# Ones-products of the softmax denominators moved beside the weighted sums, on one Trainium2 core

## The chip, the cores and the metric

The program runs on one core of one Trainium2 chip. The metric is device time in microseconds. The kernel before takes 1741.16 us (median of 3 runs, 1738.98 to 1742.28).

## The reference, cut to what matters

A two-layer network on x of 16 x 256 x 512 and a context of the same shape. Each layer is a cross attention and a feed-forward part. The change touches the attention of the second layer, eight heads of 32 channels over 512 positions:

```python
def _L1_xattn_ref(q, k, v, gamma):
    # q: layernorm(x), k and v: context, all [16, 256, 512]
    qh, kh, vh = (t.reshape(B, 8, 32, 512) for t in (q, k, v))
    qk = jnp.einsum('bhdq,bhdl->bhql', qh, kh) / sqrt(32)
    sm = jax.nn.softmax(qk, axis=-1)
    ret = jnp.einsum('bhql,bhdl->bhdq', sm, vh).reshape(B, 256, 512)
    return gamma * ret
```

The softmax denominators are the sums of exp(qk) over the 512 keys. Around it, for every batch, stand a latent attention with its own 512 x 512 softmax, a base and low-rank layer (together called the preparation of a batch here), and behind it the routing into a mixture of 64 experts, whose phase starts when all 16 batches are done.

## The kernel before, in words

**Slots.** The second attention is cut into 512 slots, 32 for a batch. A slot is one head and one block of 128 keys. Four heads form a half; four slots of four heads, one for each key block ("a step"), make 4 x 4 = 16 slots, called a quad: 32 quads in all. In slot n TensorE makes the key product (`key_chunk`, L686) and a score product 20 slots ahead of its turn (`score_chunk`, L677), whose maximum VectorE takes (L1192). ScalarE makes the exponential of the key product into `p_t` (L956), of which there are two buffers, one for each odd and even step. After each step come the weighted sums (`weighted`, L698), four products of 32 columns, one for each head, that share the array. They stand at n + 6.75 for n = 0, 4, 8, 12 of the quad, that is at slots 6.75, 10.75, 14.75 and 18.75.

**Denominators.** They are made by products with a matrix of ones, again four of 32 columns each. GpSimd adds steps 0 and 1 of a quad into `p_sum` (L1442). `sums0` (L713) multiplies `p_sum`, `sums2` the buffer of step 2 and `sums1` that of step 3 (both L720), all into one PSUM bank. ScalarE takes the logarithm of it (`sums`, L968) and the exponential of its negative (`expand`, L972). VectorE multiplies the weighted sums by that (`inv`, L1208), which frees their bank, and adds the result to x (`add`, L1214).

**Order.** Every engine executes one fixed list. `schedule` gives each piece of work a place on a common scale of slots and sorts by place, then by rank: key, score, weighted, tail and maxima, preparation, dispatch. The tail offsets count from the end of a quad (slot 16), so -4 is slot 12 and 0.25 is slot 16.25, which is also slot 0.25 of the next quad. The preparation of a batch is spread over 38 slots and its places count modulo 32; two batches' preparation overlap. Within the 32 slots of a batch, TensorE's pieces that matter here are:

- slots 11 to 15: `s3` (11, L600), `g` (11.75, L592), the maxima's transpose `max` (12, L709), from the third batch of slots on `place` (12, L750 to L753), `t0` and `t1` (13, 13.25, L606), `t2` (14.25), `lat0` (14.75, L613), `t3` (15). `t0` waits for `prob`, which ScalarE normalises in `n2`, `n3` (12.25, 12.5, L890) behind the cast of the maxima `max_hi` (12.25, L963); VectorE's reciprocals `r2`, `r3` (L1095) precede them.
- slots 19 to 24: `lat1` to `lat3` (L613), then `mean` (24.25, L620), which waits for VectorE's `moments` (place 22, L1098, L1100), itself behind ScalarE's `lat` (21.25, L897).
- slots 28 to 34: `max` (28), `o0` and `o1` (28.25, L628), which wait for ScalarE's `relu` (28, L900), and `x0`, `x1` (33, 34.25, L634), which wait for `xn20`, `xn21` (31.25, 32.25, L853).
- slots 36 to 38: `lora` (36, L642), the base products (L655) and `gated` (37, L649), which waits for VectorE's `lora2`, `gates0`, `gates1` (36.25 to 36.75) with ScalarE's `gate_exp` (36.5, L915, L916) between.

A planner (`use`, `taken`) gives banks 5 to 7 to the preparation, tail and dispatch stages in the order of TensorE's list, each time the bank that was last read earliest. So moved places also change which bank a stage gets.

Of the kernel before, what the change touches and what calls it, by code (L numbers as in the profile page):

```python
# [67 lines left out]
GPSIMD_OUT = {"rstd": 14.25, "send": 63}  # L68
SYNC_OUT = {"out": 10}

TENSOR_TAIL = {"sums0": -4, "sums2": -3.5, "sums1": 0.25}
SCALAR_TAIL = {"sums": 0.75, "expand": 2.75}
VECTOR_TAIL = {"inv": 4, "add": 5.5}

TENSOR_MAX = {"max": 1}
SCALAR_MAX = {"max": 1.25}
# [10 lines left out]
def schedule(dims, prepare, tail, maxima, dispatch, core):  # L87

    B, HALF, NHEAD, C = dims["B"], dims["HALF"], dims["NHEAD"], dims["T"] // P
    H4 = NHEAD // HALF
    QUAD, SLOTS = C * H4, NHEAD * C
    AHEAD = LEAD * H4
    out = []
    if "fill" in core:
        late = dims["NEXP"] - FIRST_FILLS
        out += [(prepare["k0"] - PREPARE, 0, ("fill", n)) for n in range(FIRST_FILLS)]
        out += [(FILL_FROM + n * FILL_SLOTS / late - PREPARE, 0, ("fill", FIRST_FILLS + n)) for n in range(late)]
    for n in range(B * SLOTS):  # L100
        if "key" in core:
            out.append((n, 0, ("key", n)))
        if "score" in core:
            out.append((n - AHEAD, 1, ("score", n)))
        if "add" in core and n // H4 % C == 1:
            out.append((n + 1, 2, ("add", n)))
        if "weighted" in core and n % H4 == 0:
            out.append((n + WEIGHTED, 2, ("pv", n // H4)))
    for quad in range(B * HALF):
        out += [(QUAD * (quad + 1) - AHEAD - 1 + o, 3, ("tail", quad, what)) for what, o in maxima.items()]  # L110
        out += [(QUAD * (quad + 1) + o, 3, ("tail", quad, what)) for what, o in tail.items()]
    for b in range(B):
        out += [(SLOTS * b - PREPARE + o, 4, ("prep", b, what)) for what, o in prepare.items()]
        for what, o in dispatch.items():
            for n in range(HALF * dims["TOPK"] if what == "send" else 1):
                out.append((SLOTS * (b + 1) + o + n, 5, ("disp", b, what, n)))
    return [(at, ev) for at, _, ev in sorted(out, key=lambda x: x[:2])]
# [22 lines left out]
def build(nc, a, out, slots_dram, dims):  # L140
# [22 lines left out]

    tensor_order = schedule(dims, TENSOR, TENSOR_TAIL, TENSOR_MAX, TENSOR_OUT, ("key", "score", "weighted"))
    scalar_order = schedule(dims, SCALAR, SCALAR_TAIL, SCALAR_MAX, SCALAR_OUT, ("key",))
    vector_order = schedule(dims, VECTOR, VECTOR_TAIL, VECTOR_MAX, VECTOR_OUT, ("score",))
    gpsimd_order = schedule(dims, GPSIMD, {}, {}, GPSIMD_OUT, ("add",))
# [1387 lines left out]
```

## Time and profile before

| | |
|---|---|
| median of the timed runs | 1741.16 us |
| span of the profiled execution | 1799.6 us |
| TensorE busy | 1593.1 us (89%) |
| VectorE busy | 1191.2 us (66%) |
| ScalarE busy | 971.3 us (54%) |
| GpSimd busy | 953.5 us (53%) |
| slots with their preparation | to about 1140 us of the span |
| expert phase | from about 1200 us on |

The profiled execution is 58 us longer than the median of the timed runs. A busy share is an average; what decides is the order within 32 slots, which repeats 14 times with full preparation.

### The profile page before, as it was taken

To read this page: it belongs to the slowest core of one execution; us is meant where nothing else is said; L and a number is where in the kernel's file an instruction comes from. 1 tells how busy PE (TensorE), PEld (TensorE's weight loads), DVE (VectorE), ACT (ScalarE), POOL (GpSimd) and SP (SyncE) were. 2 spreads that over 40 slices of the span, in tenths; PEclk is the share of its full clock that TensorE was granted. 3 is DMA by queue.
4 is the path that set the end of the run, shared out by engine and by line. 5 is a ranking of instruction groups with operands and counts; after the bars stand their busy time and mean duration, and the time that the engine had idled before them with its cause. 6 is when DMAs were issued, how large, how long until landed. Compare 5 with 4: busy or idle time off the path is not lost.

```text
span 1799.6 us, 25136 instructions
## 1 busy us (share of the span) xinstructions
PE 1593.1 (89%) x8144; PEld 1022.0 (57%) x8144; DVE 1191.2 (66%) x2674; ACT 971.3 (54%) x1938; POOL 953.5 (53%) x889
## 2 busy tenths in 40 slices
PE   5799999989999999999999988329998999999995
PEld 2444454444454454444444443229987888888884
DVE  2477778767767877877877865217765767666652
ACT  3345665655655665665665635115554555555552
POOL 4122326455464455455455446556666666666665
PEclk8889999999999999999999989659999999999997
DMA  9957654363363363352342230059999999999995
GB/s 330 303 150 254 229 144 129 121 187 112 124 210 110 116 193 103 101 168 84 89 136 65 58 99 23 21 182 245 253 255 245 254 258 247 255 250 268 245 237 82
DMA packets 148337, 311.91 MB, mean 173 GB/s; under 512 B 27674, under 2 KB 37786, under 8 KB 148208
## 3 DMA queue, kind: packets, MB, share of 16 engines
q1 hardware_dynamic: 109296, 238.89, 42.8%
q0 software_dynamic: 38912, 71.43, 18.1%
q8 instruction: 65, 1.06, 0.2%
q14 instruction: 64, 0.52, 0.1%
HBM read 141.25 MB, written 155.91 MB: 165 GB/s over the span
## 4 chain that ended last, share of the span: by engine, by line
PE 46%; DMA 20%; issue 12%; DVE 10%; another core or an unknown queue 3%; SPq 3%; ACT 3%; POOL 2%; DVEq 1%; POOLq 0%; ACTq 0%
DMA out_rows<-y_slots,row_ids 18%; PE bank L686 7%; PE bank L698 6%; PE bank L677 5%; PE bank L655 3%; PE bank L720 3%; PE bank L600 2%; DVE max_col L1192 2%; SPq L484 2%; PE bank L613 2%; PE bank L606 2%; PE bank L628 2%; POOL out_rows L1501 2%; PE bank L739 1%
## 5 line engine op out<-in xcount | busy, mean ns | idle before, releaser
L1192 DVE TENSOR_REDUCE max_col<-bank 128x1 f32<-128x512 f32 x512 | 340.2, 682 | 148.8 <-PE bank L677 142.0
L956 ACT ACTIVATE p_t<-bank 128x512 f32<-128x512 f32 x512 | 294.3, 596 | 206.7 <-PE bank L686 183.3
L1501 POOL DMA_INDIRECT out_rows<-y_slots,row_ids x128 | 222.6, 1739 | 203.3 <-DMA out_rows<-y_slots,row_ids 160.9
L1454 POOL DMA_INDIRECT slot_rows<-row,slot_i x256 | 255.0, 996 | 77.6 <-issue 76.9
L686 PE MATMUL bank<-q_stack,k_stack 98*128 98x512 f32 x512 | 277.1, 544 | 4.9 <-ACT p_t L956 4.1
L1442 POOL TENSOR_TENSOR p_sum<-p_t 128x512 f32<-128x512 f32 x128 | 168.3, 1320 | 195.9 <-ACT p_t L956 194.0
L677 PE MATMUL bank<-k_stack,q_stack 96*128 96x512 f32 x512 | 212.9, 417 | 4.6 <-DVE max_col L1192 4.3
L686 PEld LDWEIGHTS bank<-q_stack,k_stack 98*128 98x128 f32 x512 | 97.6, 192 | 191.4 <-issue 163.3
L1491 POOL TENSOR_TENSOR down_lo<-down,down_hi 96x1024 fp32r<-96x1024 f32 x64 | 188.4, 2944 | 15.3 <-DVE down_hi L1350 15.3
L1319 DVE TENSOR_TENSOR x_slots_t_lo<-bank,x_slots_t_hi 128x512 fp32r<-128x512 f32 x128 | 88.3, 690 | 160.6 <-ACT x_slots_t_hi L1008 160.6
L795 PE MATMUL bank<-gate_up_hi,x_slots_t_hi 128*128 128x384 f32 x512 | 186.1, 364 | 0.6 <-DVE x_slots_t_lo L1319 0.5
L796 PE MATMUL bank<-gate_up_lo,x_slots_t_hi 128*128 128x384 f32 x512 | 174.6, 341 | 0.0
L797 PE MATMUL bank<-gate_up_hi,x_slots_t_lo 128*128 128x384 f32 x512 | 174.5, 341 | 0.0
L1028 ACT ACTIVATE y_slots<-bank,x_slots 128x512 f32<-128x512 f32 x128 | 88.1, 688 | 128.3 <-PE bank L819 125.3
L1340 DVE TENSOR_TENSOR gate_up_lo<-gate_up,gate_up_hi 128x768 fp32r<-128x768 f32 x128 | 142.7, 1116 | 7.2 <-issue 7.2
L698 PE MATMUL bank<-p_t,v_t 128*32 128x512 f32 x1024 | 140.7, 622 | 0.2 <-DVE head_sb L1208 0.2
L784 PE MATMUL bank<-ident,x_slots 128*128 128x128 f32 x512 | 80.7, 281 | 66.1 <-DMA x_slots<-slot_rows 65.8
L655 PE MATMUL bank<-base_w,x_t 128*128 128x512 f32 x256 | 129.8, 620 | 0.0
L677 PEld LDWEIGHTS bank<-k_stack,q_stack 96*128 96x128 f32 x512 | 99.0, 194 | 53.0 <-issue 29.3
L1371 POOL TENSOR_SCALAR row_rstd<-row_mv 128x2 f32<-128x2 f32 x48 | 10.9, 228 | 199.3 <-DVE row_mv L1078 199.3
L784 PEld LDWEIGHTS bank<-ident,x_slots 128*128 128x128 f32 x512 | 62.9, 143 | 91.1 <-DMA x_slots<-slot_rows 40.0
L1038 ACT CAST gate_up_hi<-gate_up 128x768 fp32r<-128x768 f32 x128 | 105.4, 824 | 13.4 <-DMA down<-in_down 13.4
(178 smaller groups left out, 3246.5 us busy)
## 6 DMA issues: line engine op xcount, KB each, us to landing
gate_up<-in_gate_up SPq DMA_DIRECT2D x64, 768.0 KB
slot_rows<-row SPq DMA_DIRECT2D x64, 577.0 KB, 8.0
x_slots<-slot_rows SPq DMA_DIRECT2D x64, 577.0 KB
k_stack<-prob SPq DMA_DIRECT2D x192, 128.0 KB, 3.8
down<-in_down SPq DMA_DIRECT2D x64, 384.0 KB
q_stack<-x_t SPq DMA_DIRECT2D x128, 128.0 KB
x<-in_x SPq DMA_DIRECT2D x16, 512.0 KB, 3.6
ctx<-in_ctx SPq DMA_DIRECT2D x16, 512.0 KB, 4.5
```

The lines of the kernel that those rows point to most:

```text
L655: e.matmul(bank[:, :], x_t[:, k, c, :], base_w[:, c, :], start=c == 0, stop=False)
L677: e.matmul(psum[2 + n % 2][:, :], q_st[b % 2][0:SK, head, c * P:(c + 1) * P], k_st[b % 2][0:SK, head, :], start=True, stop=True).then_inc( ...
L686: e.matmul(psum[n % 2][:, :], k_st[b % 2][0:SKM, head, j * P:(j + 1) * P], q_st[b % 2][0:SKM, head, :], start=True, stop=True).then_inc(fu ...
L698: m = e.matmul(psum[4][h * DQ:(h + 1) * DQ, :], v_t[b % 2][:, j, head + h, :], p_t[step % 2][:, h, :], start=j == 0, stop=j == C - 1)
L795: e.matmul(bk[:, 0:2 * INNER], xt_hi[u % 3][:, c, :], gu_hi[nw][:, c, :], start=c == 0, stop=False)
L796: e.matmul(bk[:, 0:2 * INNER], xt_hi[u % 3][:, c, :], gu_lo[nw][:, c, :], start=False, stop=False)
L797: m = e.matmul(bk[:, 0:2 * INNER], xt_lo[u % 3][:, c, :], gu_hi[nw][:, c, :], start=False, stop=c == C - 1)
L956: e.activation(p_t[step % 2][:, h, :], psum[n % 2][:, :], ACT.Exp, scale=SCALE).then_inc(free[n % 2], 1)
L1192: e.tensor_reduce(max_col[quad % 2][:, h, c:c + 1], psum[2 + n % 2][:, :], X, ALU.max, negate=True).then_inc(free[2 + n % 2], 1)
L1454: e.indirect_dma_start(out=slots_dram, in_=rows[b % 2][:, k, :], in_offset=None, out_offset=bass.IndirectOffsetOnAxis(ap=slot_i[b % 2][:, ...
L1491: e.tensor_tensor(dn_lo[nw][:, :, :], dn[i][:, :, :], dn_hi[nw][:, :, :].bitcast(F32), ALU.subtract).then_inc(dn_lo_ok, 1)
L1501: e.indirect_dma_start(out=out, out_offset=bass.IndirectOffsetOnAxis(ap=row_ids[e_ % NI][:, q, :].bitcast(U32), axis=0), in_=ye[e_ % NY][: ...
```

## The change: three tables of places

```diff
-TENSOR_TAIL = {"sums0": -4, "sums2": -3.5, "sums1": 0.25}
-SCALAR_TAIL = {"sums": 0.75, "expand": 2.75}
-VECTOR_TAIL = {"inv": 4, "add": 5.5}
+TENSOR_TAIL = {"sums0": -1.25, "sums2": -1.25, "sums1": 2.75}
+SCALAR_TAIL = {"sums": 3.25, "expand": 3.75}
+VECTOR_TAIL = {"inv": 4.5, "add": 6}
```

No instruction is added or taken away. On TensorE `sums0` and `sums2` move from slots 12 and 12.5 to 14.75, directly behind the weighted sums of step 2, and `sums1` from 16.25 to 18.75, directly behind those of step 3. The logarithm on ScalarE moves from 16.75 to 19.25, its exponential from 18.75 to 19.75. On VectorE `inv` moves from 20 to 20.5 and `add` from 21.5 to 22.

## Rows read from the trace of the kernel before

**Rows 1.** The page: span and number of instructions.

```profile
span 1799.6 us, 25136 instructions
```

**Rows 2.** The page, chain that ended last, shares by engine.

```profile
PE 46%; DMA 20%; issue 12%; DVE 10%; another core or an unknown queue 3%; SPq 3%; ACT 3%; POOL 2%; DVEq 1%; POOLq 0%; ACTq 0%
```

**Rows 3.** Windows, 32 slots each: length, busy PE PEld DVE ACT POOL, clock, DMA.

```profile
256.96:320.06 63.10, 62.29 (x321) 31.71 (x317) 51.98 (x128) 40.49 (x81) 33.61 (x40) 1.00 0.43 130
391.62:460.45 68.83, 64.09 (x321) 32.17 (x318) 50.54 (x128) 40.29 (x82) 35.00 (x42) 0.98 0.47 148
```

**Rows 4.** Waits of PE, 130 to 1060 us: total, times, longest.

```profile
PE bank L649 <- DVE gated L1170: 20.6, 12, 3.4
PE bank L606 <- ACT prob L890: 16.3, 8, 2.9
```

**Rows 5.** Timeline of PE around one weighted sum: start, us, work, [idle before].

```profile
606.92 0.39 PE L686 MATMUL bank<-q_stack,k_stack 98*128 98x512 f32 x1
607.15 0.39 PE L677 MATMUL bank<-k_stack,q_stack 96*128 96x512 f32 x1
607.47 1.07 PE L698 MATMUL bank<-p_t,v_t 128*32 128x512 f32 x8
608.47 0.50 PE L686 MATMUL bank<-q_stack,k_stack 98*128 98x512 f32 x1
608.80 0.40 PE L677 MATMUL bank<-k_stack,q_stack 96*128 96x512 f32 x1
```

**Rows 6.** Timeline of PE in the last quad, two ones-products side by side.

```profile
1125.65 1.06 PE L713 MATMUL bank<-p_sum,ones 128*32 128x512 f32 x8
1126.51 1.07 PE L720 MATMUL bank<-p_t,ones 128*32 128x512 f32 x8
```

**Rows 7.** Timeline of PE, slot 12 to `t0` of an undisturbed batch.

```profile
255.29 0.51 PE L686 MATMUL bank<-q_stack,k_stack 98*128 98x512 f32 x1
...
256.96 0.28 PE L709 MATMUL bank<-ident,max_col 128*16 128x128 f32 x1
...
258.89 1.07 PE L606 MATMUL bank<-ident,prob 128*128 128x128 f32 x8
```

**Rows 8.** Timelines of DVE and ACT, the same stretch.

```profile
257.29 0.21 DVE L1095 RECIPROCAL exp_sum<-exp_sum 128x1 f32<-128x1 f32 x2
...
257.48 1.33 ACT L890 ACTIVATE prob<-prob,exp_sum 128x512 f32<-128x512 f32 x2
```

**Rows 9.** Timelines of ACT and PE, the same place of a disturbed batch.

```profile
394.97 0.25 ACT L963 CAST max_hi<-bank 16x128 fp32r<-16x128 f32 x1 [3.32 <-remote]
...
396.51 1.09 PE L606 MATMUL bank<-ident,prob 128*128 128x128 f32 x8 [2.74 <-ACT prob L890]
```

**Rows 10.** Timelines of PE and ACT, slots 28 to 34 (each engine's lines together).

```profile
620.54 0.27 PE L709 MATMUL bank<-ident,max_col 128*16 128x128 f32 x1
620.67 1.98 PE L628 MATMUL bank<-theta,out_w 128*128 128x512 f32 x4
...
628.48 0.60 PE L634 MATMUL bank<-ident,xn 128*128 128x128 f32 x4
...
619.83 0.63 ACT L900 ACTIVATE theta<-theta 128x512 f32<-128x512 f32 x1
...
626.81 0.81 ACT L853 ACTIVATE xn<-x,row_off,row_rstd 128x512 f32<-128x512 f32 x1
```

**Rows 11.** Timelines of DVE and PE, slots 21 to 24.

```profile
612.50 1.73 DVE L1214 TENSOR_TENSOR x<-x,head_sb 128x512 f32<-128x512 f32 x1
614.16 0.68 DVE L1192 TENSOR_REDUCE max_col<-bank 128x1 f32<-128x512 f32 x1
...
615.71 0.38 PE L620 MATMUL bank<-lat_mv,ones 128*128 128x2 f32 x2 [0.32 <-DVE lat_mv L1100]
```

**Rows 12.** Timeline of DVE, the first step of `gates0`.

```profile
637.53 0.17 DVE L1143 TENSOR_SCALAR gate_s<-gate_s 128x2 f32<-128x2 f32 x1 [0.36 <-ACT gate_s L916]
```

**Rows 13.** Windows around the wait of rows 9, columns as in rows 3.

```profile
394.00:401.00 7.00, 4.49 (x23) 2.20 (x23) 4.10 (x15) 4.13 (x8) 0.94 (x2) 0.76 0.73 254
```

## The prediction, made before the changed kernel was run

> **What bounds the kernel now.** I read the page first (span and chain), then the windows of one batch of 32 slots, then TensorE's waits, then the timelines at the places that the moved steps leave and reach. The page shows a span of 1799.6 us [rows 1] and TensorE as the largest share of the chain, 46%, but 3% (some 54 us) under an unknown queue [rows 2]. In the windows, see how little of a batch TensorE is idle: 32 slots of 63.10 us hold 62.29 us of its work at full clock, and the disturbed batch is longer by idle time, not work [rows 3]. So up to about 1140 us a batch is TensorE's own list plus a few waits at fixed places; the expert phase behind it doesn't hold any moved step. The waits are few: `gated` for VectorE, 20.6 us in 12 batches, and `t0` for the normalised probabilities, 16.3 us in 8 [rows 4]. The question is therefore not only what the moved products cost, but which waits they were covering where they stood.
>
> **What the merging removes.** Key and score products follow each other every 0.23 us. A weighted sum that follows a score starts 0.32 us after it (0.08 more), the next key product starts 1.00 us later, and the score after that 0.33 us later (0.10 more) [rows 5]. Two 32-column groups side by side, of which the trace has a case in the last quad, start 0.86 us apart [rows 6]. A group that stands alone thus costs 0.08 + 1.00 + 0.10 = 1.18 us, and one appended to another 0.86 us: 0.32 us less. For `sums0` the last part falls on the short transpose behind it and is near nothing, so it costs 1.08 and saves 0.22. For a quad that is 0.22 + 0.32 + 0.32 = 0.86 us, for 32 quads 27.5 us, if nothing else moved. The Trainium skill (TensorEngine Tiling (Array Packing), Key Properties) says that changing the tiling mode drains TensorE; by that rule alone these 27.5 us are the result, and the trace agrees on the price of a change (0.32 us). It is the first rival below.
>
> **What it uncovers at `t0` (slots 12 to 15, 14 batches).** In the undisturbed batch the key product of slot 12 starts at 255.29, the transpose of the maxima at 256.96 and `t0` at 258.89, 3.60 us after the key product [rows 7]. VectorE's two reciprocals end at 257.50 and ScalarE's two normalisations run from 257.48 to 258.81 [rows 8]: `t0` starts when they are done and TensorE arrives at the same moment. With `sums0` (1.08) and `sums2` (1.18) gone from here TensorE arrives 2.2 us sooner and waits, because the reciprocals don't depend on either. So at this place nothing is saved, the two products come back at slot 14.75 with 2 x 0.86 = 1.72 us, and `sums1` saves 0.32: +1.4 us. One batch has exactly this pattern. In the first two batches of slots, which have no `place`, the normalisations wait for the maxima's cast, which comes earlier now; I take 0.4 us off, +1.0 each. The other 11 are like rows 9: the cast of the maxima starts 3.3 us after its transpose, released by something the trace can't name, and `t0` waits up to 2.74 us. There the transpose moves 1.0 us ahead. If its signal then escapes the disturbance, `t0` starts about 1.5 us sooner and the batch ends near -0.1; if not, +1.4. The timed runs are 58 us shorter than the span, about the chain's unknown share, so most of the disturbance should be absent there and the undisturbed row is the nearer: I take 1.1. Sum: 1.4 + 2 x 1.0 + 11 x 1.1 = **15.5 us** (2.3 to 18.8).
>
> **At `mean` (slot 24.25, 14 batches).** TensorE waits 0.32 us for VectorE, whose order is `add` (612.50, 1.73 us, beside GpSimd's additions), the maximum of slot 22 (614.16), the moments [rows 11]. The input of that maximum is ready at about 613.2. After the change VectorE takes the maximum first and `add` behind it, starting about 0.7 us later than the maximum's input allowed before, so the moments come 0.7 us later and `mean` with them. The other half of the cause, `inv` half a slot later behind a logarithm and an exponential of 0.6 us each on ScalarE, still ends ahead of that maximum. If `add` ran at its undisturbed 0.66 us beside nothing, the delay would vanish; it is beside GpSimd's additions in all 14 batches, but a part of them may be missed: 0.25 to 0.7. I take 0.7: **9.8 us** (3.5 to 9.8). Queued behind `add` are the moments and two more maxima; the banks of these are free for TensorE two slots ahead.
>
> **At `o0` and `x0` (slots 28 to 34, 14 batches).** `o0` starts at 620.67; the `relu` it needs ends at 620.46 [rows 10], and that in turn stands behind the exponential of slot 28's key product. Without `sums0` TensorE would arrive 1.08 us sooner and waits them off: nothing is saved. Between `o1` and `x0` two single groups leave (2 x 1.18) and 1.72 us come in, so `x0` would start 0.64 us sooner than 628.48. Its input ended at 627.62 [rows 10], but now the key product of slot 31, whose exponential ScalarE makes first, comes 0.5 us later behind the long block, so `xn20` and `xn21` end 0.5 us later and `x1` starts where it did before. Then `sums1` adds 0.86 behind the weighted sums: +0.87 us (0.7 to 1.0), **12.2 us** (9.8 to 14).
>
> **At `gated` (slot 37, 12 batches with a wait).** `inv` leaves the place ahead of `lora`, where VectorE was idle, for one between `lora2` and `gates0`. There VectorE waited 0.36 us for ScalarE [rows 12]; `inv` takes 0.7, so 0.3 us more: **3.6 us** (0 to 3.6). `add` was hidden behind TensorE's last base products and still is.
>
> **The rest.** The last four quads have no full preparation; there the merging may bring up to 0.86 us each, I take **-2 us** (-3.5 to 0). GpSimd's next additions wait for `sums0` to have read `p_sum`; they stand 6 slots behind its new place. SyncE's store of x waits for `add` and stands 4 slots behind. The bank planner holds the sums' bank from 14.75 to 19.25 instead of 12 to 16.75, which frees one for `t0` and `t1`; two batches waited 0.7 us there, gone in the wait for `prob`. The block of three groups keeps key and score products back for 2.7 us; both followers have two banks, and I find at most 0.14 us behind it, inside the bounds.
>
> **Sum.** 15.5 + 9.8 + 12.2 + 3.6 - 2 = 39.1 us on the profiled span: 1838.7 us. The expected change is in places that the undisturbed batches show, so I carry it over whole: 1741.2 + 39.1 = **1780.3 us**, with the terms' ends +12 and +44, so 1753 to 1785.
>
> **Rivals.**
> 1. *The merging pays and the waits don't grow* (faster). 32 x 0.86 = 27.5 us less, with half of it kept 13: 1714 to 1728. It holds if the waits at `t0` and `o0` are results of TensorE's own pace, so that their inputs come sooner as well. It decides at `t0`: the inputs would have to come over 1.4 us sooner than in rows 8. Against it: the reciprocals and the `relu` stand behind work that isn't moved. For it: ScalarE's cast of the maxima comes sooner. 0.13.
> 2. *The clock falls too.* After the wait of 2.74 us the granted clock of the next stretch is 0.76, which is part at 1.2 and part at 2.4 GHz [rows 9, 13]: 3.4 us at the lower level, worth 1.7 us of work. The new wait at `t0` is about 2.0 us. If the clock falls each time, 14 x 1.7 = 24 us more, 1804; from some of the times on 1787. 0.12.
> 3. *Most of the new waiting is absorbed.* Later waits of the same batch, `gated` above all with 20.6 us, shrink as TensorE arrives later, since what they wait for hangs on transfers and not on TensorE: 14 x 1.2 us back from the sum leaves up to 1753, and down to 1745. 0.10.
> 4. *It changes nothing to be seen* (savings and waits cancel, 1738 to 1744.5). 0.06.
>
> **How the numbers follow.** The forecast case (1753 to 1787) has 0.58, and 0.01 goes to times over 1804. A measurement of this kernel tells 0.2% (3.5 us) from no change. Faster is rival 1, 0.13; the same is rival 4, 0.06; slower is all else, 0.81. For the range I leave out rival 1 and the upper end of rival 2, which together with the edge of rival 4 is under 2 in 10: 1740 to 1800 us.
>
> **What would show it.** In the profile after: groups L698, L713, L720 spaced by 0.86 us (the merging works); a wait of about 2 us at L606 in all 14 batches; L620's wait grown from 0.32 to about 1.0; L628 with a new wait of 1 us for L900; `gates0` behind L1208. The prediction is wrong if L606's wait stays under 0.6 us in undisturbed batches, if L628 shows none, or if `add` at its new place takes 0.66 us.

## The result, and the profile after

The changed kernel takes 1780.99 us (median of 4 runs, 1778.83 to 1787.3), beside 1740.46 us for the kernel before in the same session: ratio 1.0251, 95% interval 1.0225 to 1.0277, 40.5 us slower. (The ratios here and below are estimates over all runs of a comparison, with their interval; the quotient of the two medians is 1.0233.) The prediction said 1780.3 us.

The profiled execution of the kernel after has a span of 1779.8 us. That of the kernel before, on which the prediction rests, was 58 us longer than its timed runs, so I profiled the kernel before once more, beside the first experiments (run `r0_before`); its span is 1735.4 us and it is the reference for everything below. First, the page's first lines of the kernel after (busy time, share of the span, instructions):

```profile
span 1779.8 us, 25124 instructions
PE 1573.7 (88%) x8144; PEld 1027.2 (58%) x8144; DVE 1188.3 (67%) x2674; ACT 972.1 (55%) x1938; POOL 959.8 (54%) x889
```

And of the second profile of the kernel before:

```profile
span 1735.4 us, 25136 instructions
PE 1575.1 (91%) x8144; PEld 1016.7 (59%) x8144; DVE 1202.1 (69%) x2674; ACT 973.4 (56%) x1938; POOL 953.0 (55%) x889
```

TensorE's busy time is the same; 44.4 us of span were added to it as idle time. The windows of one batch of 32 slots say the same (length, busy PE PEld DVE ACT POOL, clock, DMA share, GB/s). Kernel before, an undisturbed batch:

```profile
636.41:698.84 62.43, 62.07 (x321) 31.79 (x317) 51.19 (x128) 40.49 (x81) 35.01 (x42) 1.00 0.47 140
```

Kernel after, two batches, the second with a fall of the clock:

```profile
653.64:719.01 65.37, 61.57 (x318) 32.51 (x317) 50.20 (x129) 40.37 (x82) 35.56 (x43) 1.00 0.44 133
852.55:919.72 67.17, 63.39 (x319) 33.03 (x317) 50.48 (x129) 40.47 (x82) 35.49 (x43) 0.97 0.33 98
```

The usual batch is 2.94 us longer, although the merging did take 0.5 us of TensorE's work out of it (62.07 to 61.57). The waits of TensorE show where the idle time stands, from 130 to 1060 us: total, times, longest. Kernel after, the counterpart of [rows 4]:

```profile
PE bank L606 <- ACT prob L890: 23.7, 14, 1.7
PE bank L709 <- DVE max_col L1192: 15.4, 14, 1.1
PE bank L686 <- ACT p_t L956: 7.8, 15, 3.2
PE bank L620 <- DVE lat_mv L1100: 7.0, 14, 0.5
PE bank L750 <- DVE mask L1260: 3.5, 13, 1.6
PE bank L649 <- DVE gated L1170: 1.7, 2, 0.9
```

Kernel before, second profile (the lines of 0.7 us and less are left out):

```profile
PE bank L686 <- DMA q_stack<-max_lo: 5.1, 6, 1.3
PE bank L620 <- DVE lat_mv L1100: 4.5, 14, 0.3
PE bank L686 <- ACT p_t L956: 3.2, 1, 3.2
PE bank L750 <- DVE mask L1260: 2.4, 2, 1.4
PE bank L649 <- DVE gated L1170: 2.4, 3, 1.2
```

Two new waits stand in all 14 batches: `t0` for the probabilities, 1.7 us, and the transpose of the maxima at slot 28, 1.1 us. A third comes with them: of the 15 waits for `p_t` one (3.2 us) is in both kernels, the other 14 are new, 0.33 us each on average. TensorE's timeline of the kernel after, from slot 12 on, is the counterpart of [rows 7]; the lines left out are key and score products, transposes and `place`:

```profile
653.06 0.51 PE L686 MATMUL bank<-q_stack,k_stack 98*128 98x512 f32 x1
...
656.63 1.09 PE L606 MATMUL bank<-ident,prob 128*128 128x128 f32 x8 [1.69 <-ACT prob L890]
...
658.56 1.06 PE L698 MATMUL bank<-p_t,v_t 128*32 128x512 f32 x8
659.45 1.04 PE L713 MATMUL bank<-p_sum,ones 128*32 128x512 f32 x8
660.30 1.04 PE L720 MATMUL bank<-p_t,ones 128*32 128x512 f32 x8
...
664.57 0.50 PE L686 MATMUL bank<-q_stack,k_stack 98*128 98x512 f32 x1 [0.34 <-ACT p_t L956]
```

`t0` starts 3.57 us after the key product of slot 12, where [rows 7] has 3.60: not a tenth of a microsecond was gained by taking two products out ahead of it. Behind it the two products come back at a spacing of 0.86 us. The wait of the key product of slot 18 hangs on ScalarE: it needs the exponential of slot 16, which stands behind the cast `k_hi0` (L929, from slot 15.5).

```profile
663.40 0.62 ACT L929 CAST prob<-ctx 128x512 fp32r<-128x512 f32 x1
663.92 0.59 ACT L956 ACTIVATE p_t<-bank 128x512 f32<-128x512 f32 x1
```

At slot 28 of the same batch, beside [rows 10], first TensorE, then VectorE:

```profile
677.84 0.40 PE L677 MATMUL bank<-k_stack,q_stack 96*128 96x512 f32 x1
679.34 0.27 PE L709 MATMUL bank<-ident,max_col 128*16 128x128 f32 x1 [1.09 <-DVE max_col L1192]
679.46 1.96 PE L628 MATMUL bank<-theta,out_w 128*128 128x512 f32 x4
...
677.07 0.73 DVE L1109 SCALAR_TENSOR_TENSOR theta<-theta,lat_all,ln_gamma 128x512 f32<-128x512 f32 x1
677.84 0.75 DVE L1113 SCALAR_TENSOR_TENSOR theta<-theta,lat_all,ln_beta 128x512 f32<-128x512 f32 x1
678.51 1.28 DVE L1192 TENSOR_REDUCE max_col<-bank 128x1 f32<-128x512 f32 x2
```

VectorE has no gap here: it first scales `theta`, then takes two maxima. The transpose needs the first of them (slot 27's, which takes 0.68 us and so ends at 679.19, 0.15 us before the transpose starts); the second belongs to the next quad. In `r0_before` the transpose also starts 0.15 us behind this maximum, but `sums0` fills the time before it.

### The profile page after: what moved, and what is told of

The parts are those of the page before. It is cut to its first block and busy times, and to the rows that moved or that the text cites. A ratio compares the mean times of both kernels' runs of the same rounds, so it can differ in the third digit from the quotient of the medians.

```text
span 1779.8 us, 25124 instructions
## 1 busy us (share of the span) xinstructions
PE 1573.7 (88%) x8144; PEld 1027.2 (58%) x8144; DVE 1188.3 (67%) x2674; ACT 972.1 (55%) x1938; POOL 959.8 (54%) x889
## 5 line engine op out<-in xcount | busy, mean ns | idle before, releaser
L1454 POOL DMA_INDIRECT slot_rows<-row,slot_i x256 | 260.9, 1019 | 77.0 <-issue 76.6
L1442 POOL TENSOR_TENSOR p_sum<-p_t 128x512 f32<-128x512 f32 x128 | 171.5, 1355 | 236.1 <-ACT p_t L956 235.2
L686 PE MATMUL bank<-q_stack,k_stack 98*128 98x512 f32 x512 | 280.9, 550 | 12.6 <-ACT p_t L956 12.6
L677 PE MATMUL bank<-k_stack,q_stack 96*128 96x512 f32 x512 | 212.9, 417 | 3.5 <-DVE max_col L1192 3.2
L686 PEld LDWEIGHTS bank<-q_stack,k_stack 98*128 98x128 f32 x512 | 97.2, 191 | 163.9 <-issue 125.3
L1340 DVE TENSOR_TENSOR gate_up_lo<-gate_up,gate_up_hi 128x768 fp32r<-128x768 f32 x128 | 131.2, 1025 | 7.3 <-ACT gate_up_hi L1038 7.3
L677 PEld LDWEIGHTS bank<-k_stack,q_stack 96*128 96x128 f32 x512 | 98.9, 193 | 53.8 <-issue 32.6
L655 PE MATMUL bank<-base_w,x_t 128*128 128x512 f32 x256 | 124.7, 600 | 0.0
L817 PE MATMUL bank<-down_hi,hidden_t_hi 96*128 96x512 f32 x256 | 110.5, 432 | 0.8 <-POOL down_lo L1491 0.8
```

The lines of the kernel that those rows point to most:

```text
L677: e.matmul(psum[2 + n % 2][:, :], q_st[b % 2][0:SK, head, c * P:(c + 1) * P], k_st[b % 2][0:SK, head, :], start=True, stop=True).then_inc( ...
L686: e.matmul(psum[n % 2][:, :], k_st[b % 2][0:SKM, head, j * P:(j + 1) * P], q_st[b % 2][0:SKM, head, :], start=True, stop=True).then_inc(fu ...
L1442: e.tensor_tensor(p_sum[:, h, :], p_t[(step - 1) % 2][:, h, :], p_t[step % 2][:, h, :], ALU.add).then_inc(p_sum_ok, 1)
L1454: e.indirect_dma_start(out=slots_dram, in_=rows[b % 2][:, k, :], in_offset=None, out_offset=bass.IndirectOffsetOnAxis(ap=slot_i[b % 2][:, ...
```

## The experiments

The table gives, for one undisturbed batch of each run, how much later than in `r0_before` the key product of a slot starts, counted from the key product of slot 12, in us (worked out from the timelines of L686). Each batch is compared with the batch of the same number in `r0_before`. A step between two columns is a loss at that place, or a product that moved across a column: in the runs with moved transposes (`e7`, `e10`, `e11`) slots 15 and 18 say nothing by themselves. `r0_before` itself has 62.4 us from the maxima's transpose of one undisturbed batch to that of the next.

```text
slot           15     18     19     25     29     31     35     36     43
after         1.71   0.98   1.95   2.07   0.62   2.62   2.94   2.93   2.93
e1_readers    0.00  -0.01  -0.01   0.11   1.26   1.26   1.26   1.25   1.28
e2_sums1     -0.01  -0.72   0.24   0.35   1.51   1.53   1.85   1.84   1.84
e3_sums02     1.70   1.68   1.69   1.69   0.17   2.20   2.20   2.19   2.22
e4_no_sums0   0.01   0.01   0.02   0.03   0.02   0.02   0.02   0.02   0.01
e5_readers_p -0.01  -0.02  -0.02   0.10   0.18   0.18   0.18   1.43   1.46
e6_even_only  1.71   1.69   1.70   1.70   1.70   1.72   1.71   1.70   1.70
e7_even_fill -0.95   0.10   0.10   0.11   1.19   1.20   1.19   1.19   1.18
e9_readers_t  0.01   0.02   0.03   0.14   0.23   0.23   0.23   0.22   0.41
e10_even_f_t -0.94   0.12   0.12   0.12   0.12   0.10   0.07   0.08   0.08
e11_after_f  -0.92  -1.04  -0.19  -0.07  -1.51   0.51   0.82   0.82   1.30
```

### The kernel before again, and its parts alone

`r0_before` is the unchanged kernel.

> The kernel before once more, unchanged, for a second profile of it. If the waits that a nameless source ended (3.3 us at the cast of the maxima) belong to that one profiled execution, the span is near the timed 1740 us, a batch of 32 slots takes 63 to 64 us throughout, and t0 waits for nothing in any batch. If they belong to the kernel, the span is again near 1800 us, with t0 waiting 1 to 3 us in the later batches, and the new kernel would have lost less at t0 than its own wait of 1.7 us says.

Measured: 1737.18 us, span 1735.4 us. The waits of [rows 4] at `t0` are gone, `gated` is down from 20.6 to 2.4 us.

**`e1_readers`**: the tables of ScalarE and VectorE alone.

```diff
-SCALAR_TAIL = {"sums": 0.75, "expand": 2.75}
-VECTOR_TAIL = {"inv": 4, "add": 5.5}
+SCALAR_TAIL = {"sums": 3.25, "expand": 3.75}
+VECTOR_TAIL = {"inv": 4.5, "add": 6}
```

> Only ScalarE's and VectorE's steps take their new places; TensorE's list stays as before. Theory (TensorE now waits where the ones-products stood, at t0 and at slot 28): almost nothing, 14 x 0.17 us at mean (its wait is 0.49 in the new kernel against 0.32) plus up to 4 us at gated, so 0 to +6 us, ratio 1.000 to 1.004. Rival (the later inv, add and logarithm cost it): most of the 40 us, ratio above 1.015.

Measured: 1757.68 us, ratio 1.0089 (1.006 to 1.0118), some 15.5 us: outside what was expected, under the rival. The mean (slot 25) is only 0.11 us of a batch; 1.15 us come between slots 25 and 29, at a wait that the kernel after doesn't have. TensorE's waits:

```profile
PE bank L628 <- DVE x L1123: 10.1, 12, 0.8
```

`o0` and `o1` (L628) were given one PSUM bank: the planner works from the tables, and with the readers late it took another bank for `o1`. This loss belongs to the partial edit, not to the change.

**`e2_sums1`**: `e1_readers` with TensorE's `sums1` moved too.

```diff
-TENSOR_TAIL = {"sums0": -4, "sums2": -3.5, "sums1": 0.25}
+TENSOR_TAIL = {"sums0": -4, "sums2": -3.5, "sums1": 2.75}
```

> As e1_readers, and of the ones-products only sums1 moves, beside the weighted sums of step 3. Theory: 0.32 us less in the quads without x0 and x1 behind it, up to 0.4 us more wait at x0 in the others, with the readers' 0 to 6 us on top: ratio 0.998 to 1.004, and t0 and the transpose at slot 28 wait no more than in the kernel before. Rival (merging pays, 0.32 us in each quad): 10 us less than e1_readers. Rival (the readers): as e1_readers.

Measured: 1762.88 us, ratio 1.0127 (1.0098 to 1.0157), also above what was expected; 1.15 us a batch of it are the shared bank of `e1_readers`. From slot 15 to slot 19 the moved product costs 0.24 us instead of saving 0.32. Without the 1.0 us of `sums1` ahead of it, the key product of slot 18 comes too early for ScalarE's exponential, and waits: ten waits for `p_t`, 6.6 us together, where `e1_readers` has three of 4.8 us. In the other half of the batch, from slot 31 to 35, it costs 0.32 us, at `x0` and `x1`.

**`e3_sums02`**: the other two products moved, `sums1` and the readers as before.

```diff
-TENSOR_TAIL = {"sums0": -4, "sums2": -3.5, "sums1": 0.25}
+TENSOR_TAIL = {"sums0": -1.25, "sums2": -1.25, "sums1": 0.25}
```

> Only sums0 and sums2 move, beside the weighted sums of step 2; sums1, ScalarE and VectorE stay as before. Theory: all the cover is gone from slots 12 and 28, +1.7 us a batch at t0 and +0.5 us at slot 28 (1.72 us come in, 1.18 of sums2 is saved), 14 batches, less 1 to 2 us at the end: +30 us, ratio 1.017, with t0 waiting 1.7 us and the transpose at slot 28 1.1 us as in the new kernel. Rival (merging pays): ratio 0.989. Rival (the readers): ratio 1.000.

Measured: 1776.57 us, ratio 1.02 (1.0163 to 1.0237). Four fifths of the change's loss is here, and both large waits are, of the same length as in the kernel after:

```profile
PE bank L606 <- ACT prob L890: 23.8, 14, 1.7
PE bank L709 <- DVE max_col L1192: 14.3, 14, 1.0
```

### What the products were worth where they stood

**`e4_no_sums0`**: `sums0` replaced by one product of 1 x 2, so that the denominators lack steps 0 and 1 (`sums2` then starts the sum; that line is left out here).

```diff
-                    for h in range(H4):
-                        m = e.matmul(bank[h * DQ:(h + 1) * DQ, :], ones[:, 0:DQ], p_sum[:, h, :], start=True, stop=False)
+                    for h in range(1):
+                        m = e.matmul(bank[0:1, 0:2], ones[:, 0:1], p_sum[:, h, 0:2], start=True, stop=True)
```

> The kernel of before, with sums0's four ones-products replaced by one product of 1x2, so the denominators lack the steps 0 and 1 of each quad (this part of the computation is left out; the order of everything is kept). It prices the product where it stood before. Theory, cover: in both halves of a batch sums0 stood ahead of a place where TensorE would otherwise wait (the softmax probabilities at t0, the transpose of the maxima at slot 28), so taking 1.08 us out there brings new waits of nearly the same length: 0 to 5 us less than before in 32 quads, with a wait for prob of about 1 us at the transpose t0 and one of about 1 us at the maxima's transpose of slot 28. Rival, own cost: the product costs what its spacing says wherever it stands, 32 x 1.08 = 35 us less (about 1708 us) and no new waits.

Measured: 1738.98 us beside 1737.45, ratio 1.0016 (0.999 to 1.0041). Taking 32 products of 1.08 us away brings nothing. The batch is 62.44 us long with 1.5 us less work in it than before:

```profile
887.11:949.55 62.44, 60.52 (x308) 31.65 (x306) 51.15 (x128) 40.48 (x82) 35.04 (x43) 1.00 0.38 103
```

and the waits that took the place are these:

```profile
PE bank L709 <- DVE max_col L1192: 14.3, 16, 1.3
PE bank L750 <- ACT g_sb L879: 8.2, 12, 0.7
```

At slot 28 it is the one expected. At slot 12 a wait was expected at `t0`; it stands two steps earlier, at `place` (L750), which shares a bank with `g` here as in the kernel before, and it takes up the whole product. So it is shown for both places that TensorE gains nothing by being early. That the probabilities are late as well is not shown by this run, because TensorE no longer reaches `t0` early in it; the next one shows it.

**`e6_even_only`**: `sums0` and `sums2` moved only at slots 12 to 15 (in the even quads), nothing else changed.

```diff
+EVEN_TAIL = {id(TENSOR_TAIL): {"sums0": -1.25, "sums2": -1.25, "sums1": 0.25}}
...
-        out += [(QUAD * (quad + 1) + o, 3, ("tail", quad, what)) for what, o in tail.items()]
+        part = EVEN_TAIL.get(id(tail), tail) if quad % 2 == 0 else tail
+        out += [(QUAD * (quad + 1) + o, 3, ("tail", quad, what)) for what, o in part.items()]
```

> The kernel of before, with sums0 and sums2 moved to slot -1.25 only in the even quads, whose end falls on slots 12 to 15 of a batch of 32; the odd quads (slots 28 to 31), sums1 and all readers are as before. Theory: the t0 place alone: the 14 waits of 1.7 us for prob and, behind them, the wait of the key product of slot 18 for ScalarE's exponential: 14 x 1.5 to 1.9 = 21 to 27 us more, about 1766, and the wait at the maxima's transpose of slot 28 stays absent. The rival, that the place of the odd quads carries half or more of the loss of e3_sums02 (34 us), expects 1755 to 1759.

Measured: 1765.93 us, ratio 1.0153 (1.0106 to 1.02), 26.6 us. An undisturbed batch without a clock fall gives 1.70 us, all at slot 15; 14 times that are 23.8. The 14 batches of the trace together are 23.7 us longer, but with four clock falls in them and smaller losses in the early batches, which cancel. The wait (L609 is L606 in this kernel):

```profile
PE bank L609 <- ACT prob L893: 23.7, 14, 1.7
```

The wait of the key product of slot 18, which I had expected here too, is absent: it belongs to `sums1`, not to `t0`.

### Filling the wait

**`e7_even_fill`**: `e6_even_only`, with the latent attention's transposes and `lat0` behind the block of three groups. On ScalarE their copies move too, and with them the cast `k_hi0`.

```diff
-TENSOR: "t0": 13, "t1": 13.25, "t2": 14.25, "lat0": 14.75, "t3": 15
+TENSOR: "t0": 14.8, "t1": 14.85, "t2": 15.1, "lat0": 15.5, "t3": 16.1
-SCALAR: "t0": 13.25, "t1": 13.5, "t2": 14.5, "k_hi0": 15.5
+SCALAR: "t0": 14.9, "t1": 14.95, "t2": 15.6, "k_hi0": 17.5
```

> e6_even_only, with the transposes t0 to t3, the product lat0 and ScalarE's copies of them moved behind the three neighbouring groups (t0 and t1 from slot 13 to 14.8, t2 15.1, lat0 15.5, t3 16.1). TensorE then has key, score and weighted-sum products to do while VectorE and ScalarE make the probabilities. Theory: the loss of e6_even_only is only the uncovered wait for prob, so with t0 behind the block it is gone and the merging shows its saving of about 0.5 us in each even quad: 1733 to 1742 us, ratio 0.995 to 1.000, no wait for prob at t0. Rival: the block of three groups itself costs (it keeps the key and score products of slots 15 and 16 back, and ScalarE's and VectorE's exponentials and maxima with them): then it stays at 1750 us or more, with waits for p_t or max_col behind the block.

Measured: 1754.63 us, ratio 1.0092 (1.0062 to 1.0122): missed, and in the rival's range. The wait for `prob` is gone, and with it 1.6 of the 1.70 us (0.10 at slot 19). But the merging's saving of 0.5 us doesn't show. It goes in two small waits for VectorE: in an undisturbed batch `place` starts 0.44 us behind the maxima's transpose (for the mask; 0.12 in `r0_before`) and the score product of slot 14 starts 0.41 us behind its key product (for a bank; 0.24 is usual). And 1.08 us are lost between slots 25 and 29, by the wait of `e1_readers`: the planner again gave `o0` and `o1` one bank.

```profile
PE bank L631 <- DVE x L1126: 7.6, 9, 0.8
```

**`e5_readers_pinned`**: `e1_readers`, with the banks planned from the old tables.

```diff
-    for at, ev in scalar_order + vector_order:
+    plan = schedule(dims, SCALAR, {"sums": 0.75, "expand": 2.75}, SCALAR_MAX, SCALAR_OUT, ("key",))
+    plan += schedule(dims, VECTOR, {"inv": 4, "add": 5.5}, VECTOR_MAX, VECTOR_OUT, ("score",))
+    for at, ev in plan:
```

> The readers alone moved (sums, expand, inv, add at the new slots, TensorE's table as before), as in the run e1_readers, but the PSUM banks of the preparation planned from the old slots, so that o0 and o1 no longer share one bank. Theory: of the 15 us that e1_readers was longer, the part of the shared bank (14 waits of about 0.8 us at the expansion o1) is an effect of the bank planner and goes; what is left is the mean's wait, 14 x 0.17 = 2.4 us: 1743 to 1747 us, ratio 1.000 to 1.003. Rival: the readers' places themselves cost it, because VectorE's maxima stand behind add: the time stays at about 1757, with other waits in the place of the one for the bank.

Measured: 1756.19 us, ratio 1.0107 (1.0072 to 1.0141): missed. The wait at `o1` went, but a base product (L657 here, L655 before) shares the bank of the denominators, as in the kernel before, and ScalarE now reads that one later:

```profile
PE bank L657 <- ACT sum_sb L970: 14.4, 14, 1.0
```

The time alone would have spoken for the rival, that the readers' places cost it. The column of slot 36 and this wait show that it is a shared bank once more.

**`e9_readers_tie` and `e10_even_fill_tie`**: `e1_readers` and `e7_even_fill`, with another rule for a tie between banks that the tables free at the same slot.

```diff
-            i = min((read_last[i], taken[i], i) for i in range(3))[2]
+            i = min((read_last[i], began[i], i) for i in range(3))[2]
+            began[i] = at
```

> The readers alone moved, as in e1_readers, and the bank planner's tie broken otherwise: of two banks that the tables free at the same slot it takes the one whose stage began first, instead of the one taken less often. By this o1 shares a bank with the maxima (as in the kernel before), not with o0, and no base product stands behind the logarithm in one bank. Theory: both losses seen so far with the readers moved (e1_readers at o1, e5_readers_pinned at the base products) are the shared bank, and the readers' places cost only what VectorE's order costs at the mean and behind it: 14 x 0.18 = 2.5 us, ratio 1.000 to 1.003, no wait for x at L628's line. Rival, the places themselves: 1755 or more, ratio 1.008 to 1.011, with a wait elsewhere.

> e7_even_fill with the same tie rule. Its trace was 0.11 us a batch over before at slot 24 and lost 1.09 us at o1, in the bank it shared with o0. Theory: with that gone, 14 x 0.1 = 1.5 us over before: ratio 0.999 to 1.003, which would leave of the 27 us that e6_even_only lost at t0 nothing once the products behind the block fill the wait. Rival: the block of three groups costs it: ratio 1.007 to 1.011, the wait at o1 replaced by another.

These two and the next two ran on another chip, where the kernel before took 1799.08 us (19 runs, 1785.14 to 1807.49), not 1737 to 1743 as on the first. Measured: `e9_readers_tie` 1804.48 us, ratio 1.0031 (1.0003 to 1.0059); `e10_even_fill_tie` 1775.51 us, ratio 0.9869 (0.9828 to 0.991). The first is just above what was expected (1.003). The second is far faster than expected. Its undisturbed batch is as expected, the length of [rows 3] (63.10) within a tenth:

```profile
255.58:318.76 63.18, 62.19 (x319) 31.96 (x317) 50.85 (x129) 40.33 (x82) 32.86 (x40) 1.00 0.42 134
```

What it gains are the disturbed batches. On this chip the profiles look like the first one of the kernel before [rows 4, 9]. `e9_readers_tie` waits (L608 is L606, L651 is L649):

```profile
PE bank L651 <- DVE gated L1172: 21.3, 12, 2.8
PE bank L608 <- ACT prob L892: 17.5, 9, 2.9
```

and `e10_even_fill_tie`, where `t0` stands later, waits only for `gated` (L654):

```profile
PE bank L654 <- DVE gated L1175: 19.0, 12, 3.3
```

So of its 23.6 us some 17 are, by this estimate, the waits for `prob` that came with the disturbance; no trace of the kernel before was taken on this chip, and `e9_readers_tie` stands for it. On the first chip, where the kernel before has none of these waits, I expect no difference from it; it wasn't run there.

**`e11_after_fill`**: the kernel after with the transposes of `e7_even_fill` and the tie rule. **`e12_after_fill_max`**: with the transposes of the maxima one slot later as well, and `o0`, `o1` at 29.

```diff
-TENSOR_MAX = {"max": 1}
-SCALAR_MAX = {"max": 1.25}
-VECTOR_MAX = {"max_lo": 1.5}
-SYNC_MAX = {"max": 1.75}
+TENSOR_MAX = {"max": 2}
+SCALAR_MAX = {"max": 2.25}
+VECTOR_MAX = {"max_lo": 2.5}
+SYNC_MAX = {"max": 2.75}
```

> The kernel after (all three ones-products beside the weighted sums, all readers late), with t0 to t3, lat0 and ScalarE's copies behind the block as in e7_even_fill, and the tie rule. Theory: of the batch's 2.94 us over before the 1.95 of t0 and of the key product of slot 18 go down to 0.1 to 0.4, the mean (0.1) and slots 28 to 35 (0.9) stay: 14 x 1.1 to 1.4 = 15 to 20 us over before, ratio 1.009 to 1.012, about 1755. The waits for prob and for slot 18's p_t are gone, the one for max_col at slot 28 stays. Rival, the long block is the cause: no better than 1770.

> e11_after_fill, with the transposes of the maxima one slot later (13 and 29 instead of 12 and 28, ScalarE's, VectorE's and SyncE's steps of them with it) and o0, o1 at 29, so that one more key and one more score product stand ahead of them. Theory: the wait for max_col at slot 28 (1.0 to 1.1 us) is the other uncovered wait; with 0.57 us of products ahead of it half to all of it goes: 14 x 0.3 to 0.8 = 4 to 11 us over before, ratio 1.002 to 1.007. If the merging's own saving shows beside it, ratio below 1.000. Rival: the maxima come one slot later to the next quad's products, and the wait for them at the key products of slots 16 and 32 takes the place of the one removed: ratio 1.010 or more.

Measured, beside the same 1799.08: `e11_after_fill` 1779.51 us, ratio 0.9906 (0.9871 to 0.9941), `e12_after_fill_max` 1781.25 us, ratio 0.9908 (0.9876 to 0.994). The ratios were missed for the reason given above. The batch of `e11_after_fill` is 1.30 us over `r0_before` where 1.1 to 1.4 was expected, but that agreement is luck: up to slot 36 it is 0.82 over, because at slot 19 it is 0.19 *under* where 0.1 to 0.4 over was expected, and 0.48 come behind slot 36, with a wait for `gated` that this chip's profiles have in 12 batches and those of the first chip in two or three. At slot 19, moving `sums1` beside the weighted sums now saves 0.29 us (0.10 to -0.19), close to the 0.32 of the prediction. Two things changed for it together, and no run takes them apart: the wait at `t0` is filled, and ScalarE's cast `k_hi0` no longer stands ahead of the exponential of slot 16. An undisturbed batch of each, first `e11_after_fill`:

```profile
901.62:965.34 63.72, 61.67 (x319) 32.42 (x317) 49.78 (x129) 40.47 (x82) 35.47 (x43) 1.00 0.37 102
```

then `e12_after_fill_max`:

```profile
843.06:907.01 63.95, 62.00 (x318) 32.28 (x317) 50.09 (x128) 40.59 (x81) 35.10 (x42) 1.00 0.35 104
```

The second gains nothing in the whole batch; up to slot 36 its least disturbed batches gain 0.25 us (0.5 over `r0_before` instead of 0.75). I had taken the wait for `max_col` at slot 28, 1.1 us, for one that other products can fill. Most of it they can't: VectorE is behind with all its maxima there, so the score product put ahead of the transpose waits for a free bank, which VectorE has to read first (L679 is L677 before):

```profile
865.50 0.51 PE L679 MATMUL bank<-k_stack,q_stack 96*128 96x512 f32 x1 [0.53 <-DVE max_col L1194]
```

## Why the prediction was right, and where its terms were off

The mechanism was right: the products stood where TensorE would have waited anyway. `e4_no_sums0` shows it at its plainest, `e3_sums02` and `e6_even_only` show the two places, `e7_even_fill` shows that only the uncovered wait was lost at the first. The total of 39.1 us agrees with the 40.5 measured better than its terms deserve. The account below is of two profiled executions, whose spans differ by 44.4 us; the 4 us between that and 40.5 are within the differences from run to run (the kernel before took 1733 to 1751 us beside the first experiments).

- **Merging.** Right in TensorE's work: 0.5 us less a batch, groups at 0.86 us. Of the rival that it pays, nothing is left: at the places of `sums0` and `sums2` even the filled variant is 0.1 us over before. (What of the 0.32 us is the change of the array's division, and what the order of the products, no run takes apart.)
- **`t0`.** The wait (1.69 us) and the return of both products are as worked out: +1.71 us at slot 15, where the prediction had 2 x 0.86 = 1.72. The term that failed is "`sums1` saves 0.32": `e2_sums1` shows that it costs 0.24, by the wait at slot 18, and in the kernel after the columns of slots 15 and 19 give 0.24 too (1.71 to 1.95). And I took 0.3 us off for the disturbed batches, of which the timed runs have none. So 1.95 a batch, 27.3 us in 14, where I had 15.5; my upper end was 18.8. The key product of slot 18 waits for an exponential that ScalarE makes behind the cast `k_hi0`, which I had not followed for this place.
- **`mean`.** Mis-sized the other way. The order on VectorE is as said, with `add` behind the maximum, but it took 1.11 us there, not 1.73. Kernel after:

```profile
672.45 1.11 DVE L1214 TENSOR_TENSOR x<-x,head_sb 128x512 f32<-128x512 f32 x1
674.43 0.39 PE L620 MATMUL bank<-lat_mv,ones 128*128 128x2 f32 x2 [0.51 <-DVE lat_mv L1100]
671.73 1.28 POOL L1442 TENSOR_TENSOR p_sum<-p_t 128x512 f32<-128x512 f32 x1
```

  and GpSimd beside the `add` of [rows 11] (612.50) in the kernel before:

```profile
612.40 1.28 POOL L1442 TENSOR_TENSOR p_sum<-p_t 128x512 f32<-128x512 f32 x1
```

  Both times `add` ends 0.55 us behind the end of the GpSimd addition that runs when it starts. Its duration is what is left of that addition (1.18 us before, 0.56 after) plus 0.55. Counted from slot 19, GpSimd's addition and with it `add` end 0.71 us later than in `r0_before`, but the maximum (0.60 us) no longer stands between `add` and the moments, so these come 0.11 later. The batch grows by 0.11 (the wait from 0.32 [rows 11] to 0.51, partly because the product before it is recorded as shorter): 1.5 us in 14, not 9.8, and under my lower end of 3.5. The slip was to carry one row's duration to another start, where less of GpSimd's addition was left.
- **Slots 28 to 35.** 0.87 us a batch predicted, 0.87 measured (2.07 to 2.94), 12.2 us. The wait is 1.1 us as said, but it stands one step ahead, at the maxima's transpose, and for VectorE, not at L628 for ScalarE's `relu`. I had looked at what `o0` needs and not at what the transpose in front of it needs. The `relu` ends at 679.26, the transpose starts at 679.34, so the price came out the same, by luck. The half at `x0` and `x1` was right in its mechanism too: each starts when its `xn` is done (686.85 for `x0`).

```profile
678.63 0.63 ACT L900 ACTIVATE theta<-theta 128x512 f32<-128x512 f32 x1
...
686.04 0.81 ACT L853 ACTIVATE xn<-x,row_off,row_rstd 128x512 f32<-128x512 f32 x1
...
686.90 0.66 PE L634 MATMUL bank<-ident,xn 128*128 128x128 f32 x4
```

  These waits are too short for the lists of waits; they show in the spacing, 0.37 us behind the score product instead of 0.24. By them slots 31 to 35 cost 0.32 us, in `e2_sums1` as in the kernel after, where the merging alone would save 0.32.
- **`gated`.** 3.6 us predicted, none came: in the undisturbed batch columns 36 and 43 are equal, and the waits went from 2.4 to 1.7 us. The row that showed VectorE waiting 0.36 us there [rows 12] was true, but TensorE didn't wait for it; the 20.6 us of [rows 4] were the disturbance's.
- **The clock (rival 2).** It came in part. The wait at `t0` is 1.7 us in all 14 batches, but only in four is the batch 67.0 to 67.2 us long instead of 65.4, with a lower clock in its window (0.97 in the one shown above). Behind the wait in that one stands half speed, 1.2 GHz:

```profile
857.00:859.00 2.00, 2.00 (x10) 0.99 (x12) 1.36 (x5) 1.39 (x3) 0.12 (x1) 0.50 0.90 309
```

  The four add 6.7 us together, 1.7 each, the price I had. What decides between the four and the ten stays open.
- **Absorption (rival 3).** It came in part too, and only 0.7 us of it at `gated`, in the third batch. The first seven batches grew by less than 2.94 us each (the clock's share taken off): 8.1 us less in all. In the two without `place` the wait at `t0` is worth 0.5 us less each, and the kernel before waits 5.1 us for the transfer of `q_stack`, in six of the seven, which the kernel after never does. The rest, 1.3 us, I can't assign. The 14 batches together are 40.0 us longer: 14 x 2.94 = 41.2, 6.7 of the clock, -8.1, and 0.2 in the rest. Rivals 2 and 3 happened together and cancelled.
- **The end.** I had -2 us for the last quads. The last stretch between two maxima's transposes went from 39.08 to 42.60 us, and the way from there to the first expert product is 3.7 us longer. Kernel before, then after:

```profile
1012.20:1051.28 39.08, 36.46 (x210) 16.09 (x207) 32.06 (x71) 21.65 (x44) 22.52 (x22) 1.00 0.13 42
```

```profile
1050.76:1093.36 42.60, 37.94 (x208) 16.95 (x207) 31.35 (x74) 21.43 (x43) 22.18 (x21) 0.96 0.14 44
```

  Part of it is the clock (0.96). Another part is key products waiting for ScalarE, 0.9 us in two waits before and 4.8 us in seven after, over the last quads. No run takes these two apart. About 1.4 us each came back at the start and in the expert phase, which closes the account: 40.0 + 3.5 + 3.7 - 2.8 = 44.4 us of span.
- **The sums.** Two of them were wrong without bearing on the forecast: the terms' upper ends add up to +46 us, not +44, and 14 x 1.2 us off the forecast (rival 3) lead to 1763.5, not 1753.

So `t0` was 12 us too small and the end 6 us (4.4 against -2), `mean` 8 us and `gated` 4 us too large, and absorption, which I had priced as a rival and not as a term, was 8 us against 7 of the clock. The bounds of three terms (`t0`, `mean`, the end) did not hold their values; the errors cancelled, and that is luck.

## What to carry to other kernels

A product on an engine that is the bound can still be free, when it stands where the engine would wait: price a move at its old place by what would be late without it, for every instruction between, and not by the product's duration. Whether such a wait can be filled depends on who is late: work from elsewhere filled the wait for ScalarE's probabilities, but hardly the one for VectorE, since the score product offered needed VectorE too. And where banks are given out by a plan, a moved reader changes who waits for a shared one; 1.1 to 1.3 us a batch hung on that in `e1_readers`, `e5_readers_pinned` and `e7_even_fill`, so compare the waits by name, not the times.

## What was not expected of the hardware

One kernel, on two chips, took 1737 to 1743 and 1799 us. On the slower, and in the first profile of the kernel before (its chip is not on record), ScalarE and VectorE each sat idle at a few places for a releaser that the trace can't name; from 130 to 1140 us of the first profile:

```profile
ACT max_hi L963 <- remote: 20.8, 7, 3.5
DVE lora_mid L1132 <- remote: 20.7, 7, 3.5
```

Neither `r0_before` nor the kernel after has such a line, nor any other profile from the first chip. A change of the order is worth something else there: `e10_even_fill_tie` gained 1.3%, though its undisturbed batch is no shorter. What the releaser is stays open, and the kernel after itself was not run on that chip.

The `add` on VectorE isn't slowed in proportion beside GpSimd's additions, it ends a fixed time behind one. In the profiles of the kernel before (both) and of the kernel after, 47 of the 96 `add`s start while one of GpSimd's additions (L1442) runs; all 47 end 0.55 to 0.56 us after the end of that addition, in 1.1 to 1.7 us, where the other 49 take 0.66 to 0.69.
